# Attention of an adaLN block: two heads weighed in one section of TensorE's queue, exponentials in a ring of five half heads

## The chip, the cores and the metric

The kernel runs on one core of a Trainium2 chip. Its time is the device time of one execution in microseconds (us); where several runs are given, their median is meant. Engines are called TensorE (PE in the profile, with PEld for its loads of the stationary operand), VectorE (DVE), ScalarE (ACT), GpSimd (POOL) and SyncE (SP, which here only issues DMAs).

## What is computed

The reference is one transformer block with adaptive layer norm on x of shape (8, 512, 256), float32: a norm, attention with 16 heads of width 16 and a relative bias, a gated residual, a second norm, and a mixture of eight experts of which each token takes two. The change touches attention alone, in full:

```python
qkv = x @ W_qkv + b_qkv
qkv = qkv.reshape(B, S, 3, NHEAD, D_K)
q, k, v = (qkv[:, :, 0], qkv[:, :, 1], qkv[:, :, 2])
scores = jnp.einsum('bihd,bjhd->bhij', q, k) / jnp.sqrt(jnp.float32(D_K))
scores = scores + jnp.transpose(bias, (2, 0, 1))[None]
attn = jax.nn.softmax(scores, axis=-1)
out = jnp.einsum('bhij,bjhd->bihd', attn, v).reshape(B, S, D)
return out @ W_out + b_out
```

B is 8, NHEAD 16, S 512.

## The kernel before

`adaln_block` runs four phases one after the other: `prepare` (first norm, projections of batch 0), `attention`, `route` and `experts`. In each phase every engine has its own program, and semaphores tie them. Each engine works strictly in the order in which its program is written; there is no planner.

`attention` goes through 8 batches (the first and the last are of a kind of their own) and in each through 16 heads n; h = 16b + n. One head takes these steps:

- TensorE, `score(b, n, t)`, L1183: four matmuls, one for each tile t of 128 queries, against all 512 keys, in bf16 pieces stacked to 96 rows. They write the two banks of ps_s in turn, tile t into bank t % 2. So each waits until the bias of the tile two before is done (semaphore `biased`).
- DVE, `add_bias`, L997: adds the relative bias out of s_tile, writes sn and takes the rows' extreme value into mn. Between its tiles, `between(b, n, kind)` puts other work of DVE: after tile 1 what is planned for n, after tile 3 what is planned for n + 0.5. That is the division of attention's output (`back`), the gated output (`gate_out`), the addition of v's bias (`values`), the second norm of the batch before (`moments`, `collect`, `centre` L1051, `normal` L1061) and the two largest logits.
- `lower`, subtracting the extreme value: tiles 0 and 1 by GpSimd (L835), tiles 2 and 3 by ACT (L926). GpSimd does other work between heads (`beside`: splitting q and k into bf16 parts, splitting the experts' weights L766 and L772, moving v L739, residuals).
- TensorE, `turn_scores(h, m, pair)`, L1197: 16 transposes of 128x128 in two sets of eight (pair 0 and 1), into the four banks of ps_t, one set one head later than the scores. Set 0 waits for the four `lower` of the head, and each set waits until exp has read the same half of the head before (semaphore `exped`).
- ACT, `exp(h, m, pair)`, L934: the exponential of half a head (128 x 1024) out of ps_t into pt.
- TensorE, `weigh(b, n)`, L1211: 32 small matmuls of 128x32 stationary columns and 128 moving ones; four at a time stand side by side in four column strips of the array. Two heads after the scores. It multiplies the exponentials with v (and a column of ones for the sum) into ps_o; every four heads ACT copies ps_o to ot (`outputs`, L945; semaphore `ot_out`).

pt holds two heads. exp of head g waits until head g - 2 is weighed (semaphore `weighed`).

Beside the heads, TensorE does shared pieces that all use the one bank ps_m, in the fixed order of `USES`: (n, name) with n = 1 q0, 2 k0, 3 back3, 4 turn0, 5 turn1, 6 out0, 7 back0, 8 out1, 9 q1, 10 k1, 11 back1, 12 v0, 13 v1, 14 rows0, 14.5 rows1, 15 back2, 15.5 logits. q, k and v are the next batch's projections (L1228, L1223), absent in the last batch; back3, turn, out, rows and logits belong to the batch before, absent in the first. A piece of n comes in `shared(b, n, kind)`, one of n + 0.5 at the head's end. Each waits until the result of the piece before it has been read out of ps_m (semaphore `freed`). ACT reads q, k, turn and rows (`read_shared`): those of n before its first exp of the head, those of n + 0.5 after its two `lower`.

The order of ACT in a head is: `outputs` (n = 2, 6, 10, 14), `read_shared(n)`, exp of half 0 of head h - 1, lower tile 2, lower tile 3, `read_shared(n + 0.5)`, exp of half 1 of head h - 1.

Of the kernel before, what the change touches and what calls it, by code (L numbers as in the profile page):

```python
# [12 lines left out]
ACT = mybir.ActivationFunctionType  # L13
AX = mybir.AxisListType

P = 128
B, S, D = 8, 512, 256
NH, DK = 16, 16
# [4 lines left out]
TB = S // P  # L23
# [16 lines left out]
def at_least(engine, semaphore, value):  # L40

    if not isinstance(value, int) or value > 0:
        engine.wait_ge(semaphore, value)
# [473 lines left out]
def attention(nc, ahead, choice, x, h1t, mod_rows, ext_rows, splits, w_up_t, w_down_t, w_parts, rest_rows, h2_rows, sums):  # L517
# [11 lines left out]
    with ExitStack() as ctx:  # L529
        def sb(name, shape, dt=F32):  # L530
            return ctx.enter_context(nc.sbuf_tensor("b_" + name, shape, dt))
# [5 lines left out]
            ahead.ident, ahead.flip, ahead.qf, ahead.rest, ahead.parts, ahead.qs, ahead.ks, ahead.v_next, ahead.v)  # L537
        sn = sb("sn", [P, 2, TB, S])
        mn = sb("mn", [P, 2, TB])
        pt = sb("pt", [P, 2, TB, S])  # L540
        ot = sb("ot", [P, S])
        inv = sb("inv", [P, TB, TB])
        on = sb("on", [P, TB, D])
# [12 lines left out]
        ps_t = ctx.enter_context(nc.psum_tensor("b_ps_t", [P, TB, S], F32))  # L556
# [10 lines left out]
        turned, exped, weighed = sem("turned"), sem("exped"), sem("weighed")  # L567
# [346 lines left out]
        @block.scalar  # L914
        def _(act):
            def project_out(name, done, at):

                act.wait_ge(used, at + 1)

                at_least(act, split_done, done - 1)  # L920
                ahead.project_out(act, name, ps_m[:, :]).then_inc(freed, 1)

            def lower(b, n, t):

                act.wait_ge(biased, (b * NH + n) * TB + t + 1)
                act.activation(sn[:, n % 2, t, :], sn[:, n % 2, t, :], ACT.Identity, bias=mn[:, n % 2, t:t + 1], scale=-1.0  # L926
                               ).then_inc(lower_act, 1)

            def exp(h, m, pair):

                act.wait_ge(turned, h * 2 + pair + 1)

                at_least(act, weighed, h - 1)
                act.activation(pt[:, m, 2 * pair:2 * pair + 2, :], ps_t[:, 2 * pair:2 * pair + 2, :], ACT.Exp).then_inc(exped, 1)  # L934

            def turn_out(c, at):

                act.wait_ge(used, at + 1)
                act.activation(ont[:, c, :], ps_m[:, :], ACT.Copy).then_inc(freed, 1)

            def outputs(g, at):

                act.wait_ge(weighed, g * TB + TB)
                at_least(act, used, at)
                act.activation(ot[:, :], ps_o[:, :], ACT.Copy).then_inc(ot_out, 1)  # L945

            def read_shared(b, n, kind):
                for m, u in uses_of(kind):
                    if m == n and u in FOR_NEXT[:4]:
                        project_out(u, (b + 1) * 4 + FOR_NEXT.index(u), use(b, kind, u))  # L950
                    elif m == n and u[:4] in ("turn", "rows"):
                        turn_out(int(u[4]), use(b, kind, u))

            def batch(b, kind):
                for n in range(NH):
                    h = b * NH + n

                    if n == 2 and kind != "first":
                        outputs(b * GROUPS - 1, uses_before(b, kind))
                    if n == 6:  # L960
                        outputs(b * GROUPS, 0 if kind == "first" else use(b, kind, "back3") + 1)
                    if n in (10, 14):
                        g = (n - 6) // TB
                        outputs(b * GROUPS + g, use(b, kind, f"back{g - 1}") + 1)
                    read_shared(b, n, kind)
                    if kind != "first" or n > 0:
                        exp(h - 1, (n + 1) % 2, 0)
                    for t in range(BY_POOL, TB):
                        lower(b, n, t)
                    read_shared(b, n + 0.5, kind)  # L970
                    if kind != "first" or n > 0:
                        exp(h - 1, (n + 1) % 2, 1)

            by_batches(batch)
            for pair in range(2):
                exp(B * NH - 1, 1, pair)
            act.wait_ge(weighed, B * NH)
            act.wait_ge(used, ALL_USES)
            act.activation(ot[:, :], ps_o[:, :], ACT.Copy).then_inc(ot_out, 1)
            act.wait_ge(pe_end, by_pe("turn1a"))  # L980
            act.activation(ont[:, 1, 0:S // 2], ps_s[:, 1, 0:S // 2], ACT.Copy).then_inc(act_end, 1)
            for j in range(2):
                at = slice(j * S // 2, (j + 1) * S // 2)
                act.wait_ge(pe_end, by_pe(f"rows{j}0"))
                act.activation(ont[:, 0, at], row_bank(j, 0), ACT.Copy).then_inc(act_end, 1)
# [191 lines left out]
        def _(pe):  # L1177
            def score(b, n, t):
                k = (b * NH + n) * TB + t

                at_least(pe, biased, k - 1)
                half, m = n // HALF, n % HALF
                pe.matmul(ps_s[:, t % 2, :], qs[:, half, m, t * P:(t + 1) * P], ks[:, half, m, :],  # L1183
                          start=True, stop=True).then_inc(scored, 1)

            def turn_scores(h, m, pair):


                at_least(pe, exped, (h - 1) * 2 + pair + 1)
                for t in range(TB):  # L1190
                    if pair == 0:
                        if t < BY_POOL:
                            pe.wait_ge(lower_pool, h * BY_POOL + t + 1)
                        else:
                            pe.wait_ge(lower_act, h * (TB - BY_POOL) + t - BY_POOL + 1)
                    for j in (2 * pair, 2 * pair + 1):
                        mm = pe.transpose(ps_t[:, j, t * P:(t + 1) * P], sn[:, m, t, j * P:(j + 1) * P], ident[:, :])  # L1197
                mm.then_inc(turned, 1)

            def weigh(b, n):  # L1200

                h = b * NH + n
                pe.wait_ge(exped, h * 2 + 2)
                if n % HALF == 0:
                    pe.wait_ge(v_moved, b * 2 + n // HALF + 1)
                if n % TB == 0:

                    at_least(pe, ot_out, b * GROUPS + n // TB)
                for j in range(TB):
                    for t in range(TB):  # L1210
                        mm = pe.matmul(ps_o[2 * DK * t:2 * DK * (t + 1), n % TB * P:(n % TB + 1) * P], v[:, j, n, :],  # L1211
                                       pt[:, n % 2, j, t * P:(t + 1) * P], start=(j == 0), stop=(j == TB - 1))
                mm.then_inc(weighed, 1)

            def project(b, name, at):
# [53 lines left out]
            def shared(b, n, kind):  # L1269
                for m, u in uses_of(kind):  # L1270
                    at = use(b, kind, u)
                    if m != n:
                        continue
                    if u in FOR_NEXT:
                        project(b + 1, u, at)
                    elif u == "back3":
                        back(b * GROUPS - 1, at)
                    elif u[:4] == "back":
                        back(b * GROUPS + int(u[4]), at)
                    elif u[:4] == "turn":  # L1280
                        turn_outputs(int(u[4]), at)
                    elif u[:4] == "rows":
                        turn_rows(b - 1, int(u[4]), at)
                    elif u == "logits":
                        route_rows(at)
                    else:
                        project_outputs(int(u[3]), at)
# [3 lines left out]
            def batch(b, kind):  # L1291
                for n in range(NH):
                    h = b * NH + n
                    if n % HALF == 0:
                        pe.wait_ge(stack_in[n // HALF], (b + 1) * 32 * len(Q_PART))
                    score(b, n, 0)
                    score(b, n, 1)
                    shared(b, n, kind)
                    if kind != "first" or n > 0:
                        turn_scores(h - 1, (n + 1) % 2, 0)  # L1300
                    score(b, n, 2)
                    if kind != "first" or n > 0:
                        turn_scores(h - 1, (n + 1) % 2, 1)
                    score(b, n, 3)
                    if n > 1:
                        weigh(b, n - 2)
                    elif kind != "first":
                        weigh(b - 1, n + NH - 2)
                    shared(b, n + 0.5, kind)

            by_batches(batch)
# [36 lines left out]
            for j in range(2):  # L1348
                pe.wait_ge(act_end, j + 2)
                pe.wait_ge(dve_end, by_dve(f"rows{j}"))  # L1350
                for t in (2 * j, 2 * j + 1):
                    for c in range(DC):
                        mm = pe.matmul(ps_m[:, t * NE:(t + 1) * NE], ont[:, c, t * P:(t + 1) * P], gate[:, c, :],
                                       start=(c == 0), stop=(c == DC - 1))
# [658 lines left out]
```

## Time and profile before

| | us |
|---|---|
| median of 3 runs | 1267.48 (1264.78 to 1268.91) |
| the profiled execution | 1263.28 |
| its span, first to last instruction | 1261.5 |
| TensorE busy in the span | 1104.7 (88%) |
| DVE, ACT, GpSimd busy | 784.9, 633.6, 827.2 |

The span begins with `prepare` until about 71 us; attention goes on until about 730 us, then follow `route` and `experts`. A timeline groups neighbouring instructions of one line. The duration that it gives runs from the first one's start to the last one's end, and the ends of matmuls are modelled: two that overlap in the pipeline are both shown whole. So for TensorE the starts are what counts, and a spacing is read from one start to the next.

### The profile page before, as it was taken

The numbers are of one execution on the slowest core, as the hardware profiler recorded it, in microseconds if no ns is written. First come the engines' busy times: TensorE is split into PE (matmuls) and PEld (weight loads), VectorE is DVE, ScalarE is ACT, GpSimd is POOL, SyncE is SP. The second block draws the span as 40 slices with busy tenths as digits, with TensorE's granted clock in tenths as the row PEclk, the third lists the DMA queues.
The fourth block names the chain that finished last, engine by engine and source line by source line (L and its number), as shares of the span: only waits on it lengthen the run. The fifth ranks groups of instructions, "written<-read, shape, count | busy, mean of one in ns | idle before, by whom it ended". The sixth has DMA issues, their size and how long they took to land. (4 is left out here: it accounts for less than half of the span.)

```text
span 1261.5 us, 30595 instructions
## 1 busy us (share of the span) xinstructions
PE 1104.7 (88%) x11290; PEld 880.2 (70%) x11291; DVE 784.9 (62%) x2072; ACT 633.6 (50%) x905; POOL 827.2 (66%) x923
## 2 busy tenths in 40 slices
PE   5579999999999999999999736999999999999900
PEld 3247777777777777777777624888888888888800
DVE  4646667667686676766768675545555555555567
ACT  3548777776867767777777400222222222222222
POOL 2347588686876877768857423566766666666656
PEclk9779999999999999999999955999999999999955
DMA  8967853864558536575383163242424344433363
GB/s 282 310 213 198 191 170 81 210 135 110 155 114 213 130 103 152 143 139 173 60 185 102 68 247 113 44 113 44 113 47 116 50 108 112 108 54 48 44 167 133
DMA packets 122892, 167.14 MB, mean 132 GB/s; under 512 B 13048, under 2 KB 99320, under 8 KB 122784
## 3 DMA queue, kind: packets, MB, share of 16 engines
q1 hardware_dynamic: 103200, 137.59, 39.9%
q0 software_dynamic: 19584, 28.11, 11.8%
q8 instruction: 68, 1.11, 0.4%
q14 instruction: 40, 0.33, 0.1%
HBM read 105.22 MB, written 60.44 MB: 131 GB/s over the span
## 5 line engine op out<-in xcount | busy, mean ns | idle before, releaser
L997 DVE CUSTOM_DVE_ANT_0 b_sn<-b_ps_s,s_tile 128x512 f32<-128x512 f32 x512 | 341.3, 688 | 184.1 <-PE b_ps_s L1183 180.9
L934 ACT ACTIVATE b_pt<-b_ps_t 128x1024 f32<-128x1024 f32 x256 | 259.5, 1018 | 73.5 <-PE b_ps_t L1197 73.5
L1197 PE MATMUL b_ps_t<-ident,b_sn 128*128 128x128 f32 x2048 | 267.7, 273 | 3.2 <-POOL b_sn L835 1.5
L1197 PEld LDWEIGHTS b_ps_t<-ident,b_sn 128*128 128x128 f32 x2048 | 236.7, 141 | 40.9 <-issue 10.7
L1799 ACT ACTIVATE d_g<-d_ps_u 128x512 f32<-128x512 f32 x156 | 92.8, 598 | 305.6 <-PE d_ps_u L1912 216.9
L835 POOL TENSOR_SCALAR b_sn<-b_sn,b_mn 128x512 f32<-128x512 f32 x256 | 175.5, 698 | 96.2 <-DVE b_mn L997 95.6
L926 ACT ACTIVATE b_sn<-b_sn,b_mn 128x512 f32<-128x512 f32 x256 | 181.9, 722 | 89.6 <-DVE b_mn L997 82.8
L1912 PE MATMUL d_ps_u<-d_xp,k_wu 128*128 128x256 bf16 x1776 | 201.6, 274 | 0.1
L1927 PE MATMUL d_ps_y<-k_wd,d_gp 128*128 128x256 bf16 x1776 | 199.9, 273 | 0.0
L1183 PE MATMUL b_ps_s<-s_ks,s_qs 96*128 96x512 bf16 x512 | 178.9, 386 | 23.0 <-PEq L161 12.8
L1912 PEld LDWEIGHTS d_ps_u<-d_xp,k_wu 128*128 128x128 bf16 x1776 | 173.4, 98 | 22.0 <-issue 1.0
L1927 PEld LDWEIGHTS d_ps_y<-k_wd,d_gp 128*128 128x128 bf16 x1776 | 173.7, 98 | 20.1
L1754 POOL DMA_INDIRECT sums<-d_yo,d_places x78 | 130.3, 1671 | 59.9 <-issue 27.9
L1211 PE MATMUL b_ps_o<-b_pt,s_v 128*32 128x128 f32 x4096 | 138.4, 276 | 0.1
L1211 PEld LDWEIGHTS b_ps_o<-b_pt,s_v 128*32 128x32 f32 x4096 | 104.0, 109 | 40.8 <-ACT b_pt L934 36.8
L1837 DVE CAST d_xp<-d_ps_x 128x512 bf16<-128x512 f32 x39 | 27.0, 692 | 142.1 <-PE d_ps_x L1899 134.2
L1851 DVE TENSOR_TENSOR d_gp<-d_g,d_gp 128x512 bf16<-128x512 f32 x156 | 108.7, 697 | 5.4
L1731 POOL DMA_INDIRECT k_xg<-h_rows,d_tokens x76 | 76.3, 1004 | 44.6 <-POOL d_tokens L1727 30.0
L1743 POOL DMA_INDIRECT d_gates<-gate_rows,d_places x78 | 76.2, 977 | 43.1 <-POOL d_places L1739 22.0
L1849 DVE CAST d_gp<-d_g 128x512 bf16<-128x512 f32 x156 | 70.1, 449 | 53.3 <-ACT d_g L1799 35.4
L1183 PEld LDWEIGHTS b_ps_s<-s_ks,s_qs 96*128 96x128 bf16 x512 | 43.7, 98 | 55.5 <-DVE b_mn L997 37.1
L772 POOL TENSOR_TENSOR b_w_split<-b_w_raw,b_w_split 128x1024 bf16<-128x1024 f32 x32 | 68.8, 2150 | 0.0
(238 smaller groups left out, 1167.7 us busy)
## 6 DMA issues: line engine op xcount, KB each, us to landing
w_parts<-b_w_split SPq DMA_DIRECT2D x32, 512.0 KB, 3.8
splits<-s_parts SPq DMA_DIRECT2D x32, 384.0 KB, 4.3
s_qs<-splits SPq DMA_DIRECT2D x96, 128.0 KB, 5.9
s_ks<-splits SPq DMA_DIRECT2D x96, 128.0 KB, 7.6
b_w_raw<-in_w_up_t SPq DMA_DIRECT2D x16, 512.0 KB, 11.1
b_w_raw<-in_w_down_t SPq DMA_DIRECT2D x16, 512.0 KB, 7.1
k_wu<-w_parts SPq DMA_DIRECT2D x8, 1024.0 KB
k_wd<-w_parts SPq DMA_DIRECT2D x8, 1024.0 KB
```

The lines of the kernel that those rows point to most:

```text
L835: pool.tensor_scalar(sn[:, n % 2, t, :], sn[:, n % 2, t, :], -1.0, mn[:, n % 2, t:t + 1], ALU.mult, ALU.add).then_inc(lower_pool, 1)
L926: act.activation(sn[:, n % 2, t, :], sn[:, n % 2, t, :], ACT.Identity, bias=mn[:, n % 2, t:t + 1], scale=-1.0).then_inc(lower_act, 1)
L934: act.activation(pt[:, m, 2 * pair:2 * pair + 2, :], ps_t[:, 2 * pair:2 * pair + 2, :], ACT.Exp).then_inc(exped, 1)
L997: dve.tensor_tensor_reduce(sn[:, n % 2, t, :], ps_s[:, t % 2, :], ahead.tile[:, n, at:at + S], -1.0, BIG, ALU.add, ALU.min, mn[:, n % 2, t ...
L1183: pe.matmul(ps_s[:, t % 2, :], qs[:, half, m, t * P:(t + 1) * P], ks[:, half, m, :], start=True, stop=True).then_inc(scored, 1)
L1197: mm = pe.transpose(ps_t[:, j, t * P:(t + 1) * P], sn[:, m, t, j * P:(j + 1) * P], ident[:, :])
L1211: mm = pe.matmul(ps_o[2 * DK * t:2 * DK * (t + 1), n % TB * P:(n % TB + 1) * P], v[:, j, n, :], pt[:, n % 2, j, t * P:(t + 1) * P], start= ...
L1754: pool.indirect_dma_start(sums, bass.IndirectOffsetOnAxis(ap=places[:, u, 0, i:i + 1], axis=0), yo[:, u, i, :], None, compute_op=ALU.add). ...
L1799: act.activation(g[:, j, :], ps_u[:, j, :], ACT.Gelu).then_inc(gelued, 1)
L1851: dve.tensor_tensor(gp[:, u, 1, at], g[:, j, :], gp[:, u, 0, at], ALU.subtract).then_inc(g_split, 1)
L1912: mm = pe.matmul(ps_u[:, j // 2, j % 2 * ROWS:(j % 2 + 1) * ROWS], kept.wu[:, slot, w, c, j * P:(j + 1) * P], xp[:, u, x, c * ROWS:(c + 1) ...
L1927: mm = pe.matmul(ps_y[:, i, 0:D], gp[:, u, x, j * ROWS + i * P:j * ROWS + (i + 1) * P], kept.wd[:, slot, w, j, :], start=(j == 0 and n == ...
```

## The change

In TensorE's queue the weighing of head h - 2 stood at the end of every head, behind score 3. Now even heads weigh nothing, and odd heads weigh heads h - 3 and h - 2, one right behind the other, between score 2 and score 3. In odd heads score 1 moves behind the shared piece, and score 3 stands ahead of the second set of transposes. pt becomes a ring of five half heads: half (2h + pair) lies in place (2h + pair) % 5, and exp of a half waits until the head that held that place has been weighed. Nothing else changes; the number of instructions that compute is the same.

```diff
-        pt = sb("pt", [P, 2, TB, S])
+
+        HALVES = 5
+        pt = sb("pt", [P, HALVES, 2, S])
...
-            def exp(h, m, pair):
+            def exp(h, pair):
 
                 act.wait_ge(turned, h * 2 + pair + 1)
 
-                at_least(act, weighed, h - 1)
-                act.activation(pt[:, m, 2 * pair:2 * pair + 2, :], ps_t[:, 2 * pair:2 * pair + 2, :], ACT.Exp).then_inc(exped, 1)
+
+                at_least(act, weighed, (h * 2 + pair - HALVES) // 2 + 1)
+                act.activation(pt[:, (h * 2 + pair) % HALVES, :, :], ps_t[:, 2 * pair:2 * pair + 2, :], ACT.Exp).then_inc(exped, 1)
...
                         mm = pe.matmul(ps_o[2 * DK * t:2 * DK * (t + 1), n % TB * P:(n % TB + 1) * P], v[:, j, n, :],
-                                       pt[:, n % 2, j, t * P:(t + 1) * P], start=(j == 0), stop=(j == TB - 1))
+                                       pt[:, (h * 2 + j // 2) % HALVES, j % 2, t * P:(t + 1) * P], start=(j == 0), stop=(j == TB - 1))
...
                     score(b, n, 0)
-                    score(b, n, 1)
-                    shared(b, n, kind)
+                    if n % 2 == 0:
+                        score(b, n, 1)
+                        shared(b, n, kind)
+                    else:
+                        shared(b, n, kind)
+                        score(b, n, 1)
                     if kind != "first" or n > 0:
                         turn_scores(h - 1, (n + 1) % 2, 0)
                     score(b, n, 2)
-                    if kind != "first" or n > 0:
+                    if n % 2 == 1:
+                        for m in (n - 3, n - 2):
+                            if m >= 0:
+                                weigh(b, m)
+                            elif kind != "first":
+                                weigh(b - 1, m + NH)
+                        score(b, n, 3)
                         turn_scores(h - 1, (n + 1) % 2, 1)
-                    score(b, n, 3)
-                    if n > 1:
-                        weigh(b, n - 2)
-                    elif kind != "first":
-                        weigh(b - 1, n + NH - 2)
+                    else:
+                        if kind != "first" or n > 0:
+                            turn_scores(h - 1, (n + 1) % 2, 1)
+                        score(b, n, 3)
                     shared(b, n + 0.5, kind)
```

## Rows read from the trace of the kernel before

**Rows 1.** One stretch: its length, busy PE, PEld, DVE, ACT, POOL; clock, DMA.

```profile
400.00:481.81 81.81, 79.96 (x930) 61.47 (x929) 56.76 (x169) 60.08 (x77) 62.03 (x71) 1.00 0.59 143
```

**Rows 2.** TensorE's timeline, head 4: start, duration, engine, line; idle time in brackets.

```profile
405.12 0.60 PE L1183 MATMUL b_ps_s<-s_ks,s_qs 96*128 96x512 bf16 x2
405.56 0.60 PE L1236 MATMUL b_ps_m<-ident,b_ot 128*128 128x128 f32 x4
406.00 1.04 PE L1197 MATMUL b_ps_t<-ident,b_sn 128*128 128x128 f32 x8
...
407.10 1.04 PE L1197 MATMUL b_ps_t<-ident,b_sn 128*128 128x128 f32 x8
407.97 0.38 PE L1183 MATMUL b_ps_s<-s_ks,s_qs 96*128 96x512 bf16 x1
408.28 1.08 PE L1211 MATMUL b_ps_o<-b_pt,s_v 128*32 128x128 f32 x32
409.29 0.61 PE L1183 MATMUL b_ps_s<-s_ks,s_qs 96*128 96x512 bf16 x2
```

**Rows 3.** Timeline of all engines, a score, its bias and the score two later.

```profile
472.25 0.59 PE L1183 MATMUL b_ps_s<-s_ks,s_qs 96*128 96x512 bf16 x2
...
472.85 0.69 DVE L997 CUSTOM_DVE_ANT_0 b_sn<-b_ps_s,s_tile 128x512 f32<-128x512 f32 x1 [0.22 <-PE b_ps_s L1183]
...
473.60 0.39 PE L1183 MATMUL b_ps_s<-s_ks,s_qs 96*128 96x512 bf16 x1
```

**Rows 4.** Timeline, first batch, a head without a shared piece: score 3 until transposes.

```profile
89.42 0.38 PE L1183 MATMUL b_ps_s<-s_ks,s_qs 96*128 96x512 bf16 x1
...
90.75 0.72 ACT L926 ACTIVATE b_sn<-b_sn,b_mn 128x512 f32<-128x512 f32 x1 [0.53 <-DVE b_mn L997]
...
92.44 0.86 PEld L1197 LDWEIGHTS b_ps_t<-ident,b_sn 128*128 128x128 f32 x8 [0.28 <-ACT b_pt L934]
92.44 1.09 PE L1197 MATMUL b_ps_t<-ident,b_sn 128*128 128x128 f32 x8
```

**Rows 5.** TensorE's timeline, first batch, heads 1 and 2.

```profile
80.23 0.62 PE L1183 MATMUL b_ps_s<-s_ks,s_qs 96*128 96x512 bf16 x2
81.56 0.39 PE L1183 MATMUL b_ps_s<-s_ks,s_qs 96*128 96x512 bf16 x1 [0.70 <-DVE b_mn L997]
81.79 1.88 PE L1228 MATMUL b_ps_m<-s_h,s_wqkv 128*128 128x512 f32 x4
```

**Rows 6.** Timeline, from head 14's last score to head 15's shared piece.

```profile
463.94 0.38 PE L1183 MATMUL b_ps_s<-s_ks,s_qs 96*128 96x512 bf16 x1
...
464.69 1.34 ACT L926 ACTIVATE b_sn<-b_sn,b_mn 128x512 f32<-128x512 f32 x2
...
465.95 0.60 ACT L939 ACTIVATE b_ont<-b_ps_m 128x512 f32<-128x512 f32 x1
...
466.69 0.63 PE L1236 MATMUL b_ps_m<-ident,b_ot 128*128 128x128 f32 x4 [0.34 <-ACT b_ont L939]
```

**Rows 7.** DVE's timeline, two pieces of the norm (heads 11 and 13).

```profile
448.82 1.76 DVE L1051 SCALAR_TENSOR_TENSOR h_rows<-h_rest,b_mv,b_mod 128x256 f32<-128x256 f32 x2
...
457.19 2.84 DVE L1061 SCALAR_TENSOR_TENSOR h_rows<-h_rows,b_rstd,b_mod 128x256 f32<-128x256 f32 x2
```

**Rows 8.** GpSimd's timeline at the same time.

```profile
457.20 2.15 POOL L772 TENSOR_TENSOR b_w_split<-b_w_raw,b_w_split 128x1024 bf16<-128x1024 f32 x1
```

**Rows 9.** TensorE's timelines, waits at heads 5 and 14, and at head 2 of the last batch.

```profile
415.24 0.87 PE L1197 MATMUL b_ps_t<-ident,b_sn 128*128 128x128 f32 x6 [0.16 <-POOL b_sn L835]
...
458.65 1.08 PE L1211 MATMUL b_ps_o<-b_pt,s_v 128*32 128x128 f32 x32
460.69 0.39 PE L1183 MATMUL b_ps_s<-s_ks,s_qs 96*128 96x512 bf16 x1 [0.96 <-DVE b_mn L997]
461.30 0.39 PE L1183 MATMUL b_ps_s<-s_ks,s_qs 96*128 96x512 bf16 x1 [0.22 <-DVE b_mn L997]
...
645.27 0.41 PE L1197 MATMUL b_ps_t<-ident,b_sn 128*128 128x128 f32 x2 [1.08 <-ACT b_pt L934]
```

More of the change, by code:

```diff
@@ L966, in batch @@
                     if kind != "first" or n > 0:
-                        exp(h - 1, (n + 1) % 2, 0)
+                        exp(h - 1, 0)
                     for t in range(BY_POOL, TB):
@@ L971, in batch @@
                     if kind != "first" or n > 0:
-                        exp(h - 1, (n + 1) % 2, 1)
+                        exp(h - 1, 1)
             by_batches(batch)
             for pair in range(2):
-                exp(B * NH - 1, 1, pair)
+                exp(B * NH - 1, pair)
             act.wait_ge(weighed, B * NH)
```

## Prediction

> **What bounds the kernel now.** I read the page's busy shares and slices first, then the attention stretch as a table of engines, then TensorE's timeline, because the timeline is what a reordering of TensorE's queue changes. In one batch of attention, 81.81 us from one k projection to the next, TensorE is busy 79.96 us at full granted clock, while DVE, ACT and GpSimd are busy 57 to 62 us [rows 1]. So attention is bound by TensorE's queue, but with three engines at some 70%, which hand each head to one another in a fixed order. Eight batches of this are about half of the span; route and experts behind it are untouched by the change.
>
> One head without a wait is [rows 2], 405.12 to 409.29 = 4.17 us: two scores 0.22 apart (0.60 less the 0.38 of one), a shared piece (here four transposes, 0.44), eight transposes 0.87, score, eight transposes, score, weighing. A score costs 0.22 until whatever follows it, except before a weighing: 407.97 to 408.28 is 0.31. From that last score to the next head's first is 1.32.
>
> **What the change takes away.** A weighing section of its own costs 1.32 - 0.22 = 1.10 us, since without it the next work would start 0.22 after the score. The second weighing of a joined section pays neither entry nor exit. No row shows two joined. Bounds: the 32 matmuls start within 1.08 - 0.27 = 0.81 us (the last one's own duration off), and 0.90 if the entry's 0.09 still fell on it; I take eight sets of four at the transposes' spacing (0.77 over seven steps is 0.11) = 0.87. Saved: 0.23 for each pair, between 0.20 and 0.29. Before there are 126 sections apart from one another (the last two heads are weighed together anyway), after it 63: 63 x 0.23 = **14.6 us** (12.6 to 18.3).
>
> The rows show the two edges at 0.31 - 0.22 = 0.09 and about 0.14. The Trainium skill says why there are edges (TensorEngine Tiling, Key Properties: changing the tiling mode drains the engine) and has the drain at some 128 cycles (TensorE: Matmul & The Clock Gate, Step-by-step: what each phase is for), 53 ns at 2.4 GHz. By that, an estimate, 63 x 2 x 53 ns = 6.7 us would be saved and the whole would come out 8 us later than mine; the row decides here.
>
> **The ring of half heads.** It adds no instruction. exp of a half waits for a head weighed at least two heads earlier, which by the new order lies before the transposes that feed it. I count no cost, and no gain: the wait that it replaces does not show. The second weighing of a section needs the exp of the head before, which releases TensorE 3.02 after that head's last score [rows 4]; it is reached 1.35 + 0.22 + 0.87 + 0.31 + 0.87 = 3.62 after it, so covered by 0.6 us. Were the cover gone, TensorE would wait that much in each pair.
>
> **What the new order adds.** Every odd head now holds both weighings between its third and fourth score, every even head has none. So TensorE reaches the next head 1.10 us sooner after an even head's last score, and after an odd head's last score by 1.10 less the second transposes moved there, 0.87. The other engines are not sooner. Their latencies:
> - score to bias to the score two later (two PSUM banks): score 472.25, bias from 472.85 for 0.69, next score of that bank 473.60 = **1.35** [rows 3].
> - score four to the end of the exp that frees the second transposes' banks: lowering by ACT starts 1.33 after the score (89.42 to 90.75), and the transposes released by the exp behind it come 3.02 after it (92.44), 1.09 long instead of 1.04 [rows 4], so **3.07**.
>
> Queue of an odd head: score 0, shared piece, score 1, transposes. Behind the waiting score 1 the whole TensorE queue stands.
> (a) Even to odd. Score 1 comes 0.22 + 0.22 + piece after the even head's last score, and its bank is free 1.35 after. With a projection as the piece (1.88 with its last one's duration) [rows 5] nothing is lost. With 0.44 it is 0.88, so 0.47 is lost: heads 3, 5, 7, 11 in the middle and last batches, 7, 11 and 15 in the first, 31 x 0.47 = 14.6. Without any piece it is 0.44, so 0.91 lost: heads 3, 5 of the first batch, 1, 9 of the last, 3.6. Together **+18.2**.
> (b) Head 15, which reads back a group through the one shared bank. ACT must first have copied the row transposes of 14.5, and in its queue that copy stands behind the fourth lowering. From the last score of head 14 (463.94) over two lowerings (464.69, 1.34), the copy (465.95) to the transposes back (466.69) is 2.75 [rows 6]. Before, the weighing lies in this; TensorE would have come at 0.50 less, so 0.50 is lost. After: score, rows 0.49, score = 0.93, so 1.83 lost. +1.33 in seven batches, **+9.3**.
> (c) Where two scores of a bank are only one set of transposes and two scores apart, 1.31 against 1.35: 0.04, some 60 times, **+2.5**.
> (d) Heads 12 to 14, where DVE has the norm's work in between. Before: behind two operations of 2.84 together [rows 7] score 0 of head 14 comes 460.69 - 459.46 - 0.20 = 1.02 late (459.46 is 458.65 + 1.08 - 0.27) and score 1 0.61 behind it instead of 0.22, 0.39 [rows 9]; with 0.18 at head 12 that is 1.6. After, counted from head 11's last score: fourth bias at 0.6, two centrings (1.7) [rows 7] until 2.9, two biases of head 12 until 4.1, values and a centring (1.3) until 5.4, third bias done at 6.2; TensorE, with the value projection of 1.7 and no weighing, is at head 13 at 5.5: 0.8 lost. The 2.84 then costs 0.1 to 0.9 at head 14, and 0.39 as before. I take 1.9, so +0.3 a batch; in the last batch, which has no projections there, score 2 of head 12 waits for a bias that now starts at 2.9 instead of 1.7 (1.2), and 0.7, 0.4, 0.3, 0.3 and 0.2 follow: 3.1 against 1.9. **+3.0**, with bounds of -5 (the pair of 2.84 takes 0.87, as it does one head earlier) and +9 (each takes 2.4). GpSimd's 2.15 us subtraction starts at 457.20 [rows 8] and DVE's slow operation at 457.19 [rows 7], so I hold these for coupled.
> The Trainium skill (SBUF — State Buffer, SBUF: two separate sides) has DVE and GpSimd lock one port pair for a whole instruction; that agrees with the 2.84.
> (e) Even heads without a piece: the second transposes wait for exp, 3.07 against 2.62, 0.44, where before every head without a piece lost 0.22. Five such even heads +1.1, four odd ones -0.9: **+0.2**.
> (f) Waits that go. GpSimd's lowering holds up head 5's first transposes (released at 415.24 [rows 9]) by 0.73 in six batches, 0.31 before them and 0.42 inside; score 1's own wait now gives it that time, -4.4. The last batch's head 2 waits 1.66 (645.27 [rows 9]) for the same engine, which in turn waits for head 15's weighing to free the values; that is now done a score and two sets earlier: -1.2. In the first batch head 2's second score waits 1.1 us for a bank (80.23 x2 to 81.56) [rows 5], -1.1. **-6.7**.
>
> SP and its DMAs: the order of loads and stores isn't touched, and the stacks are awaited at heads 0 and 8 alone, where no row shows a wait.
>
> **Sum.** -14.6 + 18.2 + 9.3 + 2.5 + 3.0 + 0.2 - 6.7 = **+11.9 us**. Against the profiled execution's own 1263.28 that is 1275.2. The runs' median is 1267.48, 4.2 above it; the change is the same in both, so I forecast 1267.5 + 11.9, rounded 1279 us, 0.9% slower. About 0.3% (3.8 us) is what can be told from no change.
>
> **Rivals.**
> - *The gain stands and the waits do not* (faster). For it: DVE and ACT are only 70% busy, and during a joined section of 1.7 us they catch up on everything. Against it: (a) and (b) are latencies of one score through one bank, not backlog, and catching up doesn't shorten them. With all of (a) to (d) at zero it is 1267.5 - 14.6 + 0.2 - 6.7 = 1246; it wins as soon as (a) and (b) together cost under 27.5 - 11.9 = 15.6. Chance 0.15, 1246 to 1263.
> - *About even.* (d) falls to -5 and (b) is halved because ACT reaches the copy sooner: 11.9 - 8.0 - 4.7 = -0.8, 1264 to 1271. Chance 0.12.
> - *My forecast*, slower: waits at bank and copy outweigh the edges. Price +4 to +20. Chance 0.65.
> - *GpSimd becomes the limit* as well: in even heads it has 1.1 us less before the transposes, it does not lose the 0.73 of (f), and (d) lands at +9: 4.4 + 6 more, 1286 to 1293. Point: two lowerings of 0.7 each later than the even head's last score by 1.6. Chance 0.06.
> - *A joined section has its edges after all* (the edge belongs to the wait on exp or to the first of every 32): saving near zero, 1294. Against it: the waits of score and transposes cost nothing visible in [rows 2]. Chance 0.02.
>
> **Numbers.** Likeliest 1279. Upwards the bounds of (d) and of the 0.23 give +8; downwards I go through the even case to 1263, leaving out the faster rival. Slower by over 0.3% (above 1271.3): 0.73; within: 0.12; faster: 0.15. Range 1263 to 1288.
>
> **What the changed profile would show.** Right: weighing sections of 64 matmuls in about 1.95 us; entered 0.31 after the third score, the fourth 0.20 behind the last matmul's start; the second score of heads 3, 5, 7, 11 starting 1.35 after the last score of the head before, with DVE's bias as releaser; the transposes back of head 15 waiting for ACT's copy, some 1.8; a batch of 83.0 us instead of 81.8. Wrong: TensorE's queue without idle time at those heads, or a batch under 81; a saving a pair other than 0.2 to 0.3; or new waits on exp (L934) in front of the second weighing, which I hold for covered by 0.6 us.

## The result, and the profile after

The changed kernel takes 1280.79 us in the median (1280.23 to 1283.67, four runs) against 1267.11 for the kernel before (four runs): 1.1% slower, ratio 1.0111 with a 95% interval of 1.0096 to 1.0126, +13.7 us. The forecast was +11.9 and 1279. The profiled execution took 1280.91, its span 1279.2.

The stretch of [rows 1] again, one batch, now 83.20 us long instead of 81.81 (columns as there: length, busy PE, PEld, DVE, ACT, POOL, clock, DMA):

```profile
399.99:483.19 83.20, 78.95 (x931) 61.66 (x930) 56.35 (x169) 59.13 (x77) 62.30 (x70) 1.00 0.59 141
```

TensorE is busy 1 us less in a stretch 1.4 us longer: it is idle for 4.2 us of a batch instead of 1.9. What it waits for stands in the page's groups (engine, operation, count | busy us, mean ns | idle us before it, by releaser), the kernel before first, then the changed one:

```profile
L1211 PEld LDWEIGHTS b_ps_o<-b_pt,s_v 128*32 128x32 f32 x4096 | 104.0, 109 | 40.8 <-ACT b_pt L934 36.8
L1183 PEld LDWEIGHTS b_ps_s<-s_ks,s_qs 96*128 96x128 bf16 x512 | 43.7, 98 | 55.5 <-DVE b_mn L997 37.1
...
L1214 PEld LDWEIGHTS b_ps_o<-b_pt,s_v 128*32 128x32 f32 x4096 | 107.8, 110 | 20.6 <-issue 19.9
L1186 PEld LDWEIGHTS b_ps_s<-s_ks,s_qs 96*128 96x128 bf16 x512 | 49.6, 98 | 99.6 <-DVE b_mn L1000 67.2
```

Line numbers are shifted by 3: L1186 is the scores, L1200 the transposes, L1214 the weighings. So 20 us of gaps ahead of weighings went and 44 us of gaps ahead of scores came, 30 of them released by DVE's bias (these are gaps in the weight loads, part of them beside running matmuls, so no sum of time).

The timeline of TensorE from head 2 into head 3, with which [rows 2] is to be compared (start, duration, engine, line, idle time):

```profile
412.12 0.38 PE L1186 MATMUL b_ps_s<-s_ks,s_qs 96*128 96x512 bf16 x1
412.35 1.04 PE L1200 MATMUL b_ps_t<-ident,b_sn 128*128 128x128 f32 x8
413.22 0.65 PE L1186 MATMUL b_ps_s<-s_ks,s_qs 96*128 96x512 bf16 x2
413.71 0.60 PE L1239 MATMUL b_ps_m<-ident,b_ot 128*128 128x128 f32 x4
414.57 0.39 PE L1186 MATMUL b_ps_s<-s_ks,s_qs 96*128 96x512 bf16 x1 [0.26 <-DVE b_mn L1000]
414.80 1.04 PE L1200 MATMUL b_ps_t<-ident,b_sn 128*128 128x128 f32 x8
415.68 0.38 PE L1186 MATMUL b_ps_s<-s_ks,s_qs 96*128 96x512 bf16 x1
415.99 1.96 PE L1214 MATMUL b_ps_o<-b_pt,s_v 128*32 128x128 f32 x64
417.87 0.39 PE L1186 MATMUL b_ps_s<-s_ks,s_qs 96*128 96x512 bf16 x1
418.10 0.60 PE L1200 MATMUL b_ps_t<-ident,b_sn 128*128 128x128 f32 x4
```

Two things are read here. Entered 0.31 after score 2, the joined section lets score 3 start 2.19 after it (415.68 to 417.87): 1.97 more than the 0.22 without it, where two sections apart cost 2 x 1.10. That is the 0.23 a pair. And the second score of head 3 starts at 414.57, 1.35 after head 2's last (413.22); the shared piece, four transposes, was done issuing at 414.15.

Head 15, the counterpart of [rows 6], TensorE first, then ACT:

```profile
473.91 0.38 PE L1186 MATMUL b_ps_s<-s_ks,s_qs 96*128 96x512 bf16 x1
474.13 0.60 PE L1261 MATMUL b_ps_m<-ident,h_rows 128*128 128x128 f32 x4
474.57 0.38 PE L1186 MATMUL b_ps_s<-s_ks,s_qs 96*128 96x512 bf16 x1
476.63 0.63 PE L1239 MATMUL b_ps_m<-ident,b_ot 128*128 128x128 f32 x4 [1.68 <-ACT b_ont L942]
...
474.64 1.35 ACT L928 ACTIVATE b_sn<-b_sn,b_mn 128x512 f32<-128x512 f32 x2
475.87 0.61 ACT L942 ACTIVATE b_ont<-b_ps_m 128x512 f32<-128x512 f32 x1
```

The transposes back start 2.72 after head 14's last score and 2.06 after head 15's first score, where 0.22 would do: 1.84 lost in each of seven batches.

One middle batch, two heads at a time, from the starts of the heads (us):

| heads | before | after | difference |
|---|---|---|---|
| 0, 1 | 9.23 | 9.05 | -0.18 |
| 2, 3 | 9.62 | 9.94 | +0.32 |
| 4, 5 | 9.08 | 8.65 | -0.43 |
| 6, 7 | 9.63 | 9.95 | +0.32 |
| 8, 9 | 10.92 | 10.78 | -0.14 |
| 10, 11 | 9.62 | 9.94 | +0.32 |
| 12, 13 | 12.14 | 12.37 | +0.23 |
| 14, 15 | 11.56 | 12.52 | +0.96 |

The batches one by one, from first score to first score, are the same within 0.03 us in the middle of the kernel, 81.81 before and 83.21 after (the second batch, with its first turn through these heads, 81.98 and 83.58); the first batch went from 74.00 to 75.79 and the last, until its last score, from 70.40 to 72.88. From the first score of attention to the last that is 635.42 and 648.28, **+12.9 us**. The two profiled executions are 17.6 apart: attention began 3.4 us later in the second (74.21 against 70.84), before anything that the change touches, and some 1.4 came behind its last score. In the profiles of the experiments it began between 71.1 and 75.3, at no relation to the kernel's time (at 75.3 in one that takes 1249 us). The first batch varies too: its second head took 5.6 to 7.3 us from profile to profile, and TensorE was granted the lower of its two clock levels, 1.2 GHz, in part of it: the mean from 78.00 to 83.20 was 0.67 of 2.4 GHz in the changed kernel and 0.98 in the kernel before. So sizes are best read from the middle batches.

### The profile page after: what moved, and what is told of

Same layout as the page of the kernel before. It is cut to its first block and busy times, and to the rows that moved or that the text cites. A ratio compares the mean times of both kernels' runs of the same rounds, so it can differ in the third digit from the quotient of the medians.

```text
span 1279.2 us, 30594 instructions
## 1 busy us (share of the span) xinstructions
PE 1098.6 (86%) x11290; PEld 883.3 (69%) x11291; DVE 782.3 (61%) x2072; ACT 625.9 (49%) x905; POOL 828.0 (65%) x923
## 5 line engine op out<-in xcount | busy, mean ns | idle before, releaser
L937 ACT ACTIVATE b_pt<-b_ps_t 128x1024 f32<-128x1024 f32 x256 | 256.9, 1017 | 52.1 <-PE b_ps_t L1200 52.1
L1200 PE MATMUL b_ps_t<-ident,b_sn 128*128 128x128 f32 x2048 | 266.2, 273 | 1.1 <-ACT b_pt L937 0.9
L1200 PEld LDWEIGHTS b_ps_t<-ident,b_sn 128*128 128x128 f32 x2048 | 238.4, 141 | 33.7 <-issue 12.8
L1186 PE MATMUL b_ps_s<-s_ks,s_qs 96*128 96x512 bf16 x512 | 185.5, 387 | 38.4 <-DVE b_mn L1000 22.7
L1214 PE MATMUL b_ps_o<-b_pt,s_v 128*32 128x128 f32 x4096 | 125.3, 274 | 0.1
L1214 PEld LDWEIGHTS b_ps_o<-b_pt,s_v 128*32 128x32 f32 x4096 | 107.8, 110 | 20.6 <-issue 19.9
L1186 PEld LDWEIGHTS b_ps_s<-s_ks,s_qs 96*128 96x128 bf16 x512 | 49.6, 98 | 99.6 <-DVE b_mn L1000 67.2
```

What stands on the lines that cost most here:

```text
L937: act.activation(pt[:, (h * 2 + pair) % HALVES, :, :], ps_t[:, 2 * pair:2 * pair + 2, :], ACT.Exp).then_inc(exped, 1)
```

## The experiments

The theory: the saving of 0.23 a pair is real, and what undoes it are two latencies of single items that the even heads no longer cover, the bank of the scores (a) and ACT's copy for head 15 (b). The main rival: joined sections of 1.9 us keep the other engines from keeping up, or the saving isn't one of entry and exit. Each kernel ran in rounds with the kernel before on the same chip, whose median was 1266.4 to 1269.1 there, and the ratio is to those; the last column is the length of a middle batch in the trace. Where two experiments of different rounds are compared by their medians, the difference carries up to 2.7 us of this scatter.

| kernel | median us | ratio to before (95%) | batch us |
|---|---|---|---|
| before | 1267.1 | | 81.81 |
| changed | 1280.8 | 1.0111 (1.0096 to 1.0126) | 83.21 |
| e1_split | 1291.1 | 1.0190 (1.0168 to 1.0212) | 84.72 |
| e2_no_swap | 1300.3 | 1.0261 (1.0239 to 1.0282) | 85.83 |
| e3_s3_first | 1267.1 | 1.0006 (0.9994 to 1.0019) | 82.00 |
| e4_back_late | 1271.0 | 1.0033 (1.0020 to 1.0046) | 82.10 |
| e5_both | 1261.9 | 0.9948 (0.9929 to 0.9968) | 80.94 |
| e6_best | 1249.5 | 0.9855 (0.9838 to 0.9871) | 78.79 |
| e7_ring4 | 1280.5 | 1.0106 (1.0087 to 1.0124) | 83.1 |
| e8_before_piece | 1259.3 | 0.9932 (0.9915 to 0.9948) | 80.38 |
| e9_before_pool | 1255.6 | 0.9901 (0.9877 to 0.9925) | 79.67 |
| e10_best_split | 1263.0 | 0.9955 (0.9933 to 0.9977) | 80.45 |
| e11_end | 1261.8 | 0.9955 (0.9939 to 0.9972) | 80.40 |
| e12_best_ring4 | 1248.0 | 0.9851 (0.9816 to 0.9886) | 78.79 |

### e1_split: is it entry and exit that are saved?

```diff
                             elif kind != "first":
                                 weigh(b - 1, m + NH)
-                        score(b, n, 3)
+                            if m == n - 3:
+                                score(b, n, 3)
```

> Changed kernel, but in odd heads score 3 stands between the two weighings instead of behind them. Edge theory (each weighing section on its own pays 0.09 on entry and 0.14 on exit, so 0.23 a pair): 63 pairs give back 14.5 us, 1295; the trace shows 0.31 before and 0.20 behind every weighing of 32. Rival (the second weighing was cheaper for another reason, such as less waiting, or the edges overlap with something): same time as the changed kernel, 1281.

1291.1, +10.3 on the changed kernel, where 14.5 was expected: the direction and most of the size. TensorE's timeline of this kernel, head 3:

```profile
335.79 1.08 PE L1214 MATMUL b_ps_o<-b_pt,s_v 128*32 128x128 f32 x32
336.81 0.39 PE L1186 MATMUL b_ps_s<-s_ks,s_qs 96*128 96x512 bf16 x1
337.13 1.08 PE L1214 MATMUL b_ps_o<-b_pt,s_v 128*32 128x128 f32 x32
338.14 1.09 PE L1200 MATMUL b_ps_t<-ident,b_sn 128*128 128x128 f32 x8
```

A section of 32 costs 1.01 or 1.02 from its start to that of what follows, and 0.31 or 0.32 of entry behind a score, again and again. An odd head is 0.28 longer (5.78 against 5.50), an even one 0.06 shorter (4.38 against 4.44), because score 3, now ahead of the second weighing, gives DVE the 0.04 that it lacked. That is 0.22 a pair, so the edges are there in full. What is missing went where TensorE waited for DVE's norm anyway: heads 12 and 13 together are not longer but 0.19 shorter (12.18 against 12.37), and the last batch takes what it took (72.85 against 72.88). From the first score of attention to the last the two traces are 8.0 us apart.

### e2_no_swap: the wait for the bank, doubled

```diff
-                    if n % 2 == 0:
-                        score(b, n, 1)
-                        shared(b, n, kind)
-                    else:
-                        shared(b, n, kind)
-                        score(b, n, 1)
+                    score(b, n, 1)
+                    shared(b, n, kind)
```

> Changed kernel, but odd heads have score 1 ahead of the shared piece again, as even heads do. Bank theory (score 1 can't start before 1.35 us after the even head's last score): heads with a four-transpose piece lose 0.91 instead of 0.47, heads with a projection 0.91 instead of nothing, head 15 gains 0.2; +3.7 us a middle batch, 1.6 to 3.1 in the others, about +27, 1308. Rival (the loss comes from the joined section's length, which delays the other engines): the order ahead of it changes nothing, 1281.

1300.3, +19.5, where +27 was expected. At the boundary it is as the bank theory has it, TensorE from head 0 to head 1:

```profile
412.52 0.65 PE L1186 MATMUL b_ps_s<-s_ks,s_qs 96*128 96x512 bf16 x2
413.87 0.39 PE L1186 MATMUL b_ps_s<-s_ks,s_qs 96*128 96x512 bf16 x1 [0.70 <-DVE b_mn L1000]
414.10 1.88 PE L1231 MATMUL b_ps_m<-s_h,s_wqkv 128*128 128x512 f32 x4
```

413.87 is 1.35 after 412.52, and TensorE stands still where a projection could have run. Heads 1 and 9 are longer by 0.87 each, 3, 5, 7 and 11 by 0.43. My +27 was too much mainly because of heads 12 and 13, which are 0.45 and 0.20 shorter: where everything comes later, they wait less for DVE's norm, and head 13, which has a projection too, doesn't lose the 0.91 that was put on it.

### e3_s3_first: the wait for the bank, covered

```diff
                     else:
-                        if kind != "first" or n > 0:
-                            turn_scores(h - 1, (n + 1) % 2, 1)
                         score(b, n, 3)
+                        if kind != "first" or n > 0:
+                            turn_scores(h - 1, (n + 1) % 2, 1)
```

> Changed kernel, but even heads too have score 3 ahead of the second set of transposes, so that 0.87 us of transposes lie between an even head's last score and the next head's first. Bank theory: the waits of 0.4 to 0.5 at heads 3, 5, 7 and 11 go, head 15's copy comes 0.5 sooner; -2.7 us a middle batch, -3.2 in the first, -3.5 in the last, about -23, 1258, faster than the kernel before by 9. Rival (three busy engines are the limit, and TensorE waits elsewhere instead): within 5 us of the changed kernel, the waits having moved to the transposes (on ACT or GpSimd).

1267.1, -13.7 instead of -23: the bank theory's wait is gone, but other waits took part of it. TensorE from head 2 to head 3, and then at heads 5 and 15:

```profile
320.81 0.60 PE L1186 MATMUL b_ps_s<-s_ks,s_qs 96*128 96x512 bf16 x2
321.24 1.04 PE L1200 MATMUL b_ps_t<-ident,b_sn 128*128 128x128 f32 x8
322.16 0.39 PE L1186 MATMUL b_ps_s<-s_ks,s_qs 96*128 96x512 bf16 x1
322.39 0.60 PE L1239 MATMUL b_ps_m<-ident,b_ot 128*128 128x128 f32 x4
322.83 0.38 PE L1186 MATMUL b_ps_s<-s_ks,s_qs 96*128 96x512 bf16 x1
...
331.62 0.41 PE L1200 MATMUL b_ps_t<-ident,b_sn 128*128 128x128 f32 x2 [0.19 <-POOL b_sn L837]
332.20 0.88 PE L1200 MATMUL b_ps_t<-ident,b_sn 128*128 128x128 f32 x6 [0.17 <-POOL b_sn L837]
...
383.78 0.63 PE L1239 MATMUL b_ps_m<-ident,b_ot 128*128 128x128 f32 x4 [1.68 <-ACT b_ont L942]
```

Head 3 runs through: its second score is 1.8 after head 2's last, with no gap. Heads 3, 7 and 11 are 0.43 shorter, and head 12 is 0.56 shorter, since the wait for DVE at head 13's first score is gone. But head 5 again waits 0.78 for GpSimd's lowering, the wait of [rows 9] that the changed kernel had hidden behind the wait for the bank; head 0, without a shared piece, waits 0.39 for DVE at score 3; and head 15's wait stays at 1.84. The last is my error: I took the copy to follow the lowerings, and these the scores. In head 14, ACT does two copies and an exponential ahead of the lowerings (until 381.81), so these began when ACT was free, not when the bias was done, and an earlier score moves nothing.

### e4_back_late and e5_both: the wait for ACT's copy

```diff
                     else:
-                        shared(b, n, kind)
+                        if n < 15:
+                            shared(b, n, kind)
                         score(b, n, 1)
                     if kind != "first" or n > 0:
                         turn_scores(h - 1, (n + 1) % 2, 0)
+                    if n == 15:
+                        shared(b, n, kind)
```

> Changed kernel, but TensorE does head 15's shared piece (the transposes back) after the first set of transposes instead of ahead of score 1. Copy theory (ACT's copy behind the fourth lowering frees the shared bank 2.75 us after head 14's last score): the wait of 1.84 becomes 0.31 there and 0.42 at score 1, -1.1 in seven batches, +0.4 in the first, about -7, 1273.5. Rival (head 15 is late because DVE or exp are): the wait moves on to whatever stands there next and the time stays, 1281.

1271.0, -9.8, where -7 was expected. A middle batch is 1.1 shorter, as calculated, and the traces' attention 7.6 (648.28 to 640.70); the rest of the 9.8 lies in the scatter of the medians. TensorE at head 15:

```profile
386.25 0.38 PE L1186 MATMUL b_ps_s<-s_ks,s_qs 96*128 96x512 bf16 x1
386.95 0.39 PE L1186 MATMUL b_ps_s<-s_ks,s_qs 96*128 96x512 bf16 x1 [0.32 <-DVE b_mn L1000]
387.17 1.04 PE L1200 MATMUL b_ps_t<-ident,b_sn 128*128 128x128 f32 x8
388.31 0.63 PE L1239 MATMUL b_ps_m<-ident,b_ot 128*128 128x128 f32 x4
```

Of the 1.84 some 0.7 is left: score 1 comes 0.70 after score 0 instead of 0.22, at its bank, and the transposes back come 1.14 after the first of the eight instead of 0.87. So what head 15 waited for in the changed kernel was ACT's copy, and of that wait an order of TensorE's queue alone takes 1.1 away.

e5_both makes this edit and that of e3 together.

> Score 3 first in even heads, and head 15's transposes back behind its first set of transposes: the two edits together on the changed kernel. They act at different places, so latencies add: against score 3 first alone (1267) the wait of 1.84 at head 15 becomes some 0.7, -1.1 in seven batches, -7.8, 1259.5, 7 faster than the kernel before. If the three other engines were the limit, the second edit would bring nothing on top of the first: 1267.

1261.9, where 1259.5 was expected; the middle batch falls by 1.06 on top of e3, as calculated. The two waits are independent of one another, and joined weighing is now 0.5% faster than the kernel before.

### e8_before_piece, e9_before_pool, e6_best: GpSimd beside DVE's norm

The move is made on the kernel before in e8, with weighing left as it was:

```diff
-                if n == 13.5:
-                    piece_low(b, 2)
                 if n == 14 and not first:
                     rest_of(b - 1, 0)
+                if n == 14:
+                    piece_low(b, 2)
```

> The kernel before, with GpSimd's weight subtraction of head 13.5 moved behind the first part of head 14's rest and nothing else. Coupling theory (DVE's norm pair takes 2.84 instead of 0.87 because GpSimd's two-input operation runs beside it): the pair takes 0.9, the waits of 1.02 and 0.39 at head 14 go, -1.4 in six batches and -0.5 in the last, about -9, 1257.5. Rival (the pair is slow for its own operands): 1266.5 as before. This sizes term (d) of the prediction.

1259.3, -8.2. In the kernel before, DVE's pair took 2.84 [rows 7] while GpSimd subtracted [rows 8]; the changed kernel showed the same (2.93). In e8, DVE's row and GpSimd's:

```profile
456.38 0.87 DVE L1061 SCALAR_TENSOR_TENSOR h_rows<-h_rows,b_rstd,b_mod 128x256 f32<-128x256 f32 x2
...
460.15 2.14 POOL L772 TENSOR_TENSOR b_w_split<-b_w_raw,b_w_split 128x1024 bf16<-128x1024 f32 x1
```

The same instruction, apart from GpSimd's, takes 0.87 for two. In the kernel before, one by one, the first of the two took 2.45 and the second 0.47, as either does in e8, while GpSimd's took 2.15 there and 2.14 here. That one of them waited about as long as GpSimd's ran (the pair is 1.97 longer, beside 2.15) agrees with the rule of the Trainium skill that the two engines take turns on one port pair for whole instructions (SBUF — State Buffer, SBUF: two separate sides).

e9 adds the second move, which takes GpSimd's residual out of the way of head 5; e6 makes both moves on e5:

```diff
-                if n == 4 and not first:
+                if n == 4.5 and not first:
                     residual(b - 1, 0)
-                if n == 4.5 and not first:
+                if n == 5 and not first:
                     residual(b - 1, 1)
```

> The kernel before with both moves in GpSimd's queue (subtraction of head 13.5 behind head 14's rest; residual at 4.5 and 5), every head weighing alone. Against the subtraction's move alone (1259.3) head 5's wait of 0.73 goes in six batches: -4.4, 1255. So with the same GpSimd queue, joined weighing in the order without bank waits (1249.5) is worth 5.5 us net. If joined weighing were worth nothing once GpSimd is out of the way, this run comes to 1250.

> The two edits of the run before it, and two moves in GpSimd's queue: the residual goes from heads 4 and 4.5 to 4.5 and 5 (it held up head 5's first transposes by 0.78), and the weight subtraction of head 13.5 goes behind the first part of head 14's rest, away from DVE's norm. If the 2.84 us pair of DVE is slow because GpSimd runs beside it, it takes 0.87 and the waits of 1.02 and 0.39 at head 14 go; -0.78 - 1.4 in six batches, -13, 1247. If it is slow for itself, only the first: -4.7, 1255.

e9 took 1255.6 and e6 1249.5, where 1255 and 1247 were expected. With GpSimd's queue the same, joined weighing in a good order is worth 6.1 us, 0.9 a middle batch (79.67 to 78.79). That is under half of the 14.6 that entries and exits give: e6 still loses 0.39 at head 0, 0.77 at head 15 (now for GpSimd's lowering, behind the moved subtraction) and the 0.04 at boundaries.

### e10_best_split: entry and exit again, where little else waits

The edit of e1 on e6.

> The kernel of 1249.5 (score 3 first in even heads, head 15's transposes back late, GpSimd's two moves) with score 3 between the two weighings of an odd head. Edge theory: 63 x 0.23 = 14.5, less what still waits at head boundaries (0.04 in 55 places): +12 to +14.5, 1262 to 1264. Splitting the changed kernel itself gave only +10.3, since there the earlier score 3 also shortened a wait of DVE's; here these waits are gone, so more of it should show. Rival: edges of 0.1 each pair at most, 1256.

1263.0, +13.5. Where fewer waits are left to swallow it, 63 pairs give back 0.21 each, and so does the trace: a middle batch is 1.66 longer, over eight pairs. The rule of the Trainium skill that a change of tiling mode drains the engine (TensorEngine Tiling, Key Properties) agrees in its kind; the estimate of 6.7 us from the 128 cycles that the Trainium skill gives for a drain (TensorE: Matmul & The Clock Gate, Step-by-step: what each phase is for) is half of what e10 shows.

### e11_end: does the place of the section matter?

```diff
-                        for m in (n - 3, n - 2):
-...
-                        score(b, n, 3)
                         turn_scores(h - 1, (n + 1) % 2, 1)
+                        score(b, n, 3)
+                        for m in (n - 3, n - 2):
+...
```

> The kernel of 1249.5 with both weighings at the odd head's end, behind its fourth score, instead of between third and fourth. If the place of the joined section hardly matters as long as 1.35 us of work lie between an even head's last score and the next score 1: the same within 3 us, rather 1 faster, since the 0.04 waits at the odd heads' ends go. Rival (the place between the scores is what covers DVE's and ACT's latencies): slower by 0.4 or more in 63 odd heads, 1275 or more.

1261.8, +12.3 on e6: wrong, my order-of-work argument left out exp. TensorE in head 3 of this kernel, then its weight load for the same transposes:

```profile
324.15 0.38 PE L1186 MATMUL b_ps_s<-s_ks,s_qs 96*128 96x512 bf16 x1
324.67 1.09 PE L1200 MATMUL b_ps_t<-ident,b_sn 128*128 128x128 f32 x8
...
324.67 0.86 PEld L1200 LDWEIGHTS b_ps_t<-ident,b_sn 128*128 128x128 f32 x8 [0.52 <-ACT b_pt L937]
```

The second transposes of an odd head now come right behind score 2 and wait for the exponential of the even head before, 0.30 and 0.06 more inside them, at heads 3, 5, 7 and 11. Between the scores, the section stood ahead of these transposes and covered that. Head 13's first score, too, comes 0.4 later, released by DVE's bias. So the place matters, half as much as the rival said: it is another single latency, from score 3 to exp.

### e7_ring4 and e12_best_ring4: the ring

`HALVES = 4` instead of 5, once in the changed kernel and once in e6.

> Changed kernel with a ring of four half heads instead of five, the same storage as before. exp of an odd head then waits for the first weighing of its own head, some 1.5 us after score 2, and ends 2.5 after it, while the fourth lowering can't start before 3.5. Cover theory: no cost, 1281 within 2. Rival (the fifth half is what keeps ACT from waiting for the joined section): exp0 is up to 1.5 us later in 63 odd heads and all of it reaches TensorE, up to +60.

> The kernel of 1249.5 with a ring of four half heads, the storage that the kernel before has. exp of an odd head's first half waits for the first weighing of that head; the fourth lowering, which starts 1.33 after score 3, still hides it, as in the ring of four on the changed kernel: 1249.5 within 2. Rival (in a queue with fewer waits the fifth half does matter): 0.3 or more in 63 odd heads, 1268 or more.

1280.5 and 1248.0: no cost either time. ACT does wait. In the changed kernel its first exponential of head 3 follows the exponential before it at once (two in 1.92); with four halves it comes later, released by the weighing, and the next lowering behind it:

```profile
415.18 1.92 ACT L937 ACTIVATE b_pt<-b_ps_t 128x1024 f32<-128x1024 f32 x2
...
416.49 1.01 ACT L937 ACTIVATE b_pt<-b_ps_t 128x1024 f32<-128x1024 f32 x1
418.50 1.03 ACT L937 ACTIVATE b_pt<-b_ps_t 128x1024 f32<-128x1024 f32 x1 [1.00 <-PE b_ps_o L1214]
419.42 0.71 ACT L928 ACTIVATE b_sn<-b_sn,b_mn 128x512 f32<-128x512 f32 x1
```

The first row is the changed kernel's, the others e7's. Nobody behind it needs it sooner: a middle batch takes 83.1 against 83.2, and 78.79 with five halves and with four. The fastest kernel of this study thus has the storage of the kernel before; between e6 and e12, 1249.5 and 1248.0, their intervals don't tell.

## Why the prediction was right, step by step

- **The saving.** 0.23 a pair was inferred from two edges in [rows 2], with no row that showed two weighings joined. The trace has 2.19 from score to score, as 0.22 + 2 x 1.10 - 0.23 adds up; e10 gives 13.5 us back of the 14.6.
- **(a) The bank, 1.35 us** [rows 3]. Found at 413.22 to 414.57 in the changed kernel and doubled and removed by e2 and e3. The 0.47 is 1.35 - 0.88, as forecast. The rival that catching up would hide it fell: e2 and e3 change the order around one score and leave the joined section alone, and the time moves by +19.5 and -13.7.
- **(b) Head 15.** 1.84 measured, 1.83 forecast. The size is right, but the chain was told wrongly: it was put as starting at head 14's last score, and e3, which moves that score ahead, left the wait as it was. It starts in ACT's own queue, whose copies and exponentials let the lowerings begin 0.75 after that score in the kernel before (463.94 to 464.69) and 0.73 after it in the changed one (473.91 to 474.64). That the two agree, so that the 2.75 could be carried over, is luck.
- **(c), (e)** are as small as they were put.
- **(d) DVE's norm.** 1.9 a batch as forecast, but divided otherwise: 0.56 at head 13 (0.8 forecast), 1.02 at head 14's first score (0.1 to 0.9, I took 0.7) and 0.35 at its second (0.39). TensorE and DVE of the changed kernel:

```profile
462.48 0.38 PE L1186 MATMUL b_ps_s<-s_ks,s_qs 96*128 96x512 bf16 x1
463.30 0.39 PE L1186 MATMUL b_ps_s<-s_ks,s_qs 96*128 96x512 bf16 x1 [0.44 <-DVE b_mn L1000]
...
470.67 0.39 PE L1186 MATMUL b_ps_s<-s_ks,s_qs 96*128 96x512 bf16 x1 [0.86 <-DVE b_mn L1000]
471.28 0.39 PE L1186 MATMUL b_ps_s<-s_ks,s_qs 96*128 96x512 bf16 x1 [0.22 <-DVE b_mn L1000]
...
467.07 2.93 DVE L1064 SCALAR_TENSOR_TENSOR h_rows<-h_rows,b_rstd,b_mod 128x256 f32<-128x256 f32 x2
```

  That the pair would stay coupled to GpSimd was argued from two starting times; e8 has shown for the kernel before that it was so.
- **(f) The waits that go** went: heads 4 and 5 became 0.43 shorter together, where saving 0.23, losing 0.47 at the bank and 0.04 and dropping 0.73 make -0.45. e3 brought the same wait back, which shows that it was covered and not cured. The first batch's wait was misread: the 1.1 is the whole distance from head 2's first score to its second (80.23 + 0.62 - 0.38 = 80.47, and 81.56 [rows 5]), and 0.22 of it is there without a wait. So 0.87 could go; the changed kernel still waits 0.38 there, and some 0.5 was saved.
- **The ring** costs and brings nothing, as put; e7 goes further than the forecast, since even the fourth half would have done.
- **Sizes that were off.** A middle batch became 1.40 longer instead of 1.2 (83.0 was forecast, 83.21 came), the first 1.8 and the last 2.5, where the forecast's terms give some 0.8 and 3.5. In the first the misread wait is part of it. In the last the 0.47 of (a) was put on heads 3 and 11 in full, but they lost 0.07 and 0.15, since TensorE had waited 0.4 and 0.3 for DVE at the score just before. Together +12.9 in attention against 11.9; so the total is nearer to the forecast than its parts are, which is luck too. The other 0.8 up to the medians' 13.7 is within what the runs scatter.

Still open: why the start of attention varies by 4 us from one kernel's profile to another's; no run was made for that.

## What to carry to other kernels

An engine that is 98% busy in its own queue can still lose time by being given less to do at a place: the work taken away was the cover of somebody's latency. Before moving a block, list for each pair of neighbours the latency that it covers (here 1.35 us score to score through DVE, 1.33 + 0.72 = 2.05 to the end of the last lowering, 3.0 to the transposes that the exponential behind it releases) and see that enough work stays between. And where waits sit behind one another, removing one uncovers the next: e3 alone brought 1.2 us a batch instead of 2.7, since it uncovered head 5's wait for GpSimd and left head 15's. With e4's edit and GpSimd's two moves, which go at those, the batch fell by 4.4.

## What the runs showed of the hardware

- 64 matmuls of 32 stationary columns in one run cost 1.88 us from the first one's start to that of the next score; two runs of 32 cost 1.01 each, and an entry of 0.31 instead of 0.22 twice.
- Eight transposes that follow such a section directly (338.14 in e1) take 1.09 us instead of 1.04. So do those that follow a wait, as in [rows 4] and at 324.67 in e11; directly behind a score they take 1.04. It isn't a price of the section alone.
- Two two-input DVE operations that take 0.87 us together took 2.84 beside a 2.15 us two-input operation of GpSimd, 2.45 of it in the first alone, and moving GpSimd's away took 8 us off the kernel before.
